# Three more broadcasts of dt per tile in the first and the last block of a state-space and experts kernel

## The chip, the cores and the metric

The kernel runs on one core of a Trainium2 chip. The metric is the device time in microseconds. The engines are TensorE (PE, matmuls; PEld is its weight load), VectorE (DVE), ScalarE (ACT), GpSimd (POOL) and SyncE (SP, which here issues most DMAs). TensorE's clock has two levels, 1.2 and 2.4 GHz; a granted clock of 1.00 in the profile is the higher, 0.50 the lower.

## The reference

For x of 2 x 1024 tokens and 256 channels, with xn = layernorm(x), the result is x + ssm(xn) + ffn(xn).

```
# ssm(x): D = 256 channels, N = 64 states
xn = layernorm(x) * norm_w + norm_b
delta, B, C = split(xn @ x_proj_w.T)
delta = softplus(delta @ dt_proj_w.T + dt_proj_b)          # dt
h[t] = exp(dt[t] * A) * h[t-1] + dt[t] * B[t] * xn[t]       # per channel and state
y[t] = sum over states of h[t] * C[t % 64]
return (y + x * D_param) @ out_proj_w.T
# ffn(x): a shared relu^2 MLP (512) plus 6 of 64 experts per token (relu^2, inner size 128),
# chosen from 4 of 8 groups by sigmoid scores
```

## The kernel before

The recurrence is done by VectorE's scan instruction over 1024 time steps. A **tile** is two channels with their 64 states (128 partitions) and one of the two sequences: 256 tiles in 8 blocks of 32. In `body`, `it` is the block and `s` the tile within it; `c` is a tile that an engine works ahead on. The steps of a tile are:

- TensorE copies the dt of its two channels to all 128 partitions (`bcast_dt`, L1331). dt was split earlier into three bf16 parts. `spread(g, c, bank)` (L1326) multiplies 24 rows of parts (tile PK) by a selection matrix (`sel`) into one PSUM bank of 512 columns; g = 0 and 1 are the two halves of dt's 1024 time steps, g = 2 and 3 those of g = dt * xn. The groups use different quarters of the array's rows. For dt the two halves go to the banks 0 and 1 or 2 and 3, by turns. `bcast_dt` first waits for `scan_done`: the scan of tile c-2 must have left these banks.
- ScalarE makes exp(dt * A) in place there (`decay`, L820).
- TensorE copies g (`bcast_g`) and VectorE multiplies it by B into U (`product`, L1126 for both halves at once, L1131 for one). In blocks 1 to 6 and the first tiles of block 7, three of four products are done by GpSimd instead (L656), with g from DRAM or from ScalarE's copy.
- VectorE scans (L1149) into H and increments `scan_done`.
- After each group of 8 tiles TensorE sums over the states (`y_rows`, L1317, 32 columns of the array each) in three runs of 24, 20 and 20 matmuls, at s % 8 = 1, 3 and 5 of the next group. Each fp32 matmul is two records in the trace.

The order is written out by hand, in straight loops over Python numbers, one instruction stream per engine with semaphores between them. At step s TensorE does `bcast_dt` for tile s+2, then what is due of the experts or of y, then `bcast_g` for tile s+4 (where VectorE does the product), then other work. In block 0 that other work is the shared MLP of `shared_step` (L1232 up-projections, then L1238, L1243 and L1244 for one block of 128 output rows, 14 records) at even s up to 14, while GpSimd issues the rest of 96 indirect DMAs that sort the tokens by expert (`scatter`, L642, three per scan). Blocks 1 to 6 hold the experts' matmuls (L1387, L1395, L1430). In block 7 GpSimd gathers the experts' rows back by 96 indirect DMAs (`gather`, L679), and TensorE and VectorE sum them (`add_row`, L1421; `combine`, L1170; `add_sum`, L1185). The gathers wait for these sums, two to three row blocks back. At the end TensorE projects y (L1446) and the result is stored.

Of the kernel before, what the change touches and what calls it, by code (L numbers as in the profile page):

```python
# [32 lines left out]
BLK = 8  # L33
# [25 lines left out]
PARTS = 3  # L59
ROWS = PARTS * 2 * SUB  # L60
RING = 18


def state_space_and_experts(nc, x, xprojT, dtT, vecs, A_l, outT, gateT, gbias, w_up, w_down, w_exp, out):
# [5 lines left out]
    with ctx:  # L70
# [3 lines left out]
        def sem(name):  # L74
            return ctx.enter_context(nc.semaphore(name))
# [186 lines left out]
        s_y = [sem(f"y_{k}_loaded") for k in ("first_half", "second_half", "last_block", "last_groups")]  # L262
        s_g = [sem(f"rows_gathered{b}") for b in range(RING)]
        s_os = [sem(f"out_stored{b}") for b in range(2)]

        def row(n):

            n %= RING
            return WE[:, n // 4, n % 4 // 2, n % 2 * D:(n % 2 + 1) * D] if n < 12 else XG[:, (n - 12) // 2, n % 2, :]

        def at_least_0(value):

            return max(value, 0) if isinstance(value, int) else value
# [84 lines left out]
        def sums(t):  # L358

            return ps[:, 6, 0:D]  # L360
# [237 lines left out]
        def _(pool):  # L598
# [73 lines left out]
            def gather(n):  # L672
# [4 lines left out]
                elif t >= 3:  # L677
                    pool.wait_ge(comb, added(t - 3, k))
                pool.indirect_dma_start(row(n), None, yg_d,  # L679
                                        bass.IndirectOffsetOnAxis(ap=slot[:, k, t:t + 1].bitcast(u32), axis=0))\  # L680
                    .then_inc(s_g[n % RING], 16)

# [226 lines left out]
        def _(dve):  # L909
# [252 lines left out]
            def combine(t, k):  # L1162

                n = t * TOPK + k
                dve.wait_ge(s_g[n % RING], 16 * (n // RING + 1))
                if t == 0 and k == ON_PE:
# [44 lines left out]
        def _(pe):  # L1211
# [109 lines left out]
            def parts_for(it, c):  # L1321

                q = c // SUB
                pe.wait_ge(s_pk[q % NPK], (it * (SL // SUB // NPK) + q // NPK + 1) * 16)

            def spread(g, c, bank):  # L1326

                return mm(ps[:, bank, :], sel[32 * g:32 * g + ROWS, c % SUB, :],  # L1328
                          PK[32 * g:32 * g + ROWS, c // SUB % NPK, :], start=True, stop=True)

            def bcast_dt(it, c):  # L1331
                parts_for(it, c)
                pe.wait_ge(scan_done, at_least_0(it * SL + c - 1))
                spread(0, c, 2 * (c % 2))
                spread(1, c, 2 * (c % 2) + 1).then_inc(dt_bcast, 1)

# [23 lines left out]
            def body(it, moe):  # L1360
                for s in range(SL):
# [3 lines left out]
                    if not beyond(it, s + DLEAD):  # L1365
                        bcast_dt(it, s + DLEAD)
# [45 lines left out]
            def add_row(t, k):  # L1412
# [6 lines left out]
                pe.wait_ge(scaled_ident, t * ON_PE + k + 1)  # L1419
                pe.wait_ge(s_g[n % RING], 16 * (n // RING + 1))  # L1420
                ins = mm(sums(t), scaled[(t * ON_PE + k) % len(scaled)], row(n), start=(k == 0), stop=(k == ON_PE - 1))  # L1421
# [13 lines left out]
            for c in range(DLEAD):  # L1435
                bcast_dt(0, c)
# [69 lines left out]
```

## Time and profile before

| | us |
|---|---|
| three runs | 1054.78, 1041.98, 1053.79 |
| median | 1053.79 |
| the profiled execution: time | 1045.13 |
| its span | 1043.4 |
| block 0 (first scan at 170.16) | 156 |
| blocks 1 to 6 (326 to 862.4) | 536 |
| block 7 (862.4 to 1016.1) | 154 |

Over the span TensorE is busy for 807.5 us (77%), VectorE for 869.9 us (83%), ScalarE for 576.3 us and GpSimd for 571.3 us. The mean granted clock is 0.838.

In the timelines of the profile a row gives the start, the duration, the engine, the line, the operation, what it writes and reads, and how many instructions were merged; in brackets stands how long the engine was idle before, and what ended it. "issue" is a wait for nothing that the profile shows, "remote" one whose releaser it could not tell. The ends of matmuls are modelled: when a result is really there is told by the engine that waits for it.

### The profile page before, as it was taken

To read this page: it belongs to the slowest core of one execution; us is meant where nothing else is said; L and a number is where in the kernel's file an instruction comes from. 1 tells how busy PE (TensorE), PEld (TensorE's weight loads), DVE (VectorE), ACT (ScalarE), POOL (GpSimd) and SP (SyncE) were. 2 spreads that over 40 slices of the span, in tenths; PEclk is the share of its full clock that TensorE was granted. 3 is DMA by queue.
4 is the path that set the end of the run, shared out by engine and by line. 5 is a ranking of instruction groups with operands and counts; after the bars stand their busy time and mean duration, and the time that the engine had idled before them with its cause. 6 is when DMAs were issued, how large, how long until landed. Compare 5 with 4: busy or idle time off the path is not lost.

```text
span 1043.4 us, 19216 instructions
## 1 busy us (share of the span) xinstructions
PE 807.5 (77%) x6887; PEld 505.5 (48%) x6888; DVE 869.9 (83%) x725; ACT 576.3 (55%) x897; POOL 571.3 (55%) x381
## 2 busy tenths in 40 slices
PE   2967954477445898899998998988896856788788
PEld 3633641144113565566665665665664533344346
DVE  7798899555589999989998998989896999687873
ACT  3552234222225787778777787878785754233440
POOL 5002257554535765756756765756654599555640
PEclk9988985557567999999998999989998967565659
DMA  9579317222535999999999999999999862334322
GB/s 332 188 247 341 113 60 252 86 76 73 166 100 149 255 279 271 276 289 300 293 294 265 279 306 283 271 275 289 268 310 293 230 167 70 96 104 131 99 66 86
DMA packets 178206, 217.33 MB, mean 208 GB/s; under 512 B 50465, under 2 KB 137378, under 8 KB 177890
## 3 DMA queue, kind: packets, MB, share of 16 engines
q1 hardware_dynamic: 168898, 190.93, 64.7%
q0 software_dynamic: 9216, 25.18, 7.8%
q8 instruction: 57, 0.93, 0.4%
q14 instruction: 35, 0.29, 0.1%
HBM read 144.61 MB, written 71.30 MB: 207 GB/s over the span
## 4 chain that ended last, share of the span: by engine, by line
PE 29%; SPq 16%; DVE 12%; issue 11%; DMA 8%; another core or an unknown queue 4%; ACT 3%; POOL 2%; DVEq 0%; ACTq 0%; POOLq 0%
PE ps L1317 11%; DVE H L1149 9%; DMA WE<-w_exp_dram 7%; PE ps L1328 5%; SPq L444 5%; SPq L493 3%; PE ps L1421 3%; SPq L498 3%; PE ps L1387 3%; PE ps L1430 2%; DVE U L1126 2%; ACT ps L820 2%; PE ps L1395 1%; POOL U L656 1%
## 5 line engine op out<-in xcount | busy, mean ns | idle before, releaser
L1149 DVE TENSOR_TENSOR_SCAN H<-ps,U 128x1024 f32<-128x1024 f32 x256 | 581.4, 2284 | 32.6 <-ACT ps L820 27.3
L820 ACT ACTIVATE ps<-ps,Acur 128x1024 f32<-128x1024 f32 x256 | 278.9, 1090 | 263.4 <-PE ps L1328 190.9
L656 POOL TENSOR_TENSOR U<-X,B 128x1024 f32<-128x1024 f32 x100 | 237.2, 2372 | 183.7 <-DMA X<-g_d 126.4
L1328 PE MATMUL ps<-PK,sel 24*128 24x512 bf16 x824 | 153.4, 436 | 146.9 <-DVE H L1149 71.4
L1317 PE MATMUL ps<-H,CB 128*32 128x128 f32 x4096 | 247.7, 395 | 8.7 <-issue 8.5
L1317 PEld LDWEIGHTS ps<-H,CB 128*32 128x32 f32 x4096 | 145.2, 130 | 93.2 <-issue 39.7
L1328 PEld LDWEIGHTS ps<-PK,sel 24*128 24x128 bf16 x824 | 44.1, 93 | 259.5 <-issue 255.1
L642 POOL DMA_INDIRECT xg_d<-XN,slot x96 | 98.3, 1024 | 94.9 <-DVE H L1149 40.4
L1126 DVE TENSOR_TENSOR U<-ps,B 128x1024 f32<-128x1024 f32 x57 | 68.9, 1209 | 77.8 <-remote 45.6
L656 POOL TENSOR_TENSOR U<-GS,B 128x1024 f32<-128x1024 f32 x50 | 119.6, 2391 | 17.4 <-DVE H L1149 13.6
L1387 PE MATMUL ps<-XT,WE 128*128 128x128 f32 x640 | 90.8, 287 | 21.1 <-DMA WE<-w_exp_dram 21.1
L1387 PEld LDWEIGHTS ps<-XT,WE 128*128 128x128 f32 x640 | 86.1, 200 | 31.4 <-issue 28.4
L1430 PE MATMUL ps<-WE,AS 128*128 128x256 f32 x320 | 90.5, 405 | 0.0
L679 POOL DMA_INDIRECT WE<-yg_d,slot x66 | 62.9, 954 | 40.5 <-issue 19.7
L1131 DVE TENSOR_TENSOR U<-ps,B 128x512 f32<-128x512 f32 x98 | 65.5, 668 | 14.7 <-PE ps L1328 14.7
L1430 PEld LDWEIGHTS ps<-WE,AS 128*128 128x128 f32 x320 | 54.2, 189 | 22.3 <-issue 18.1
L872 ACT COPY GS<-ps 128x512 f32<-128x512 f32 x100 | 59.8, 598 | 0.4 <-PE ps L1328 0.4
L1395 PE MATMUL ps<-ident,XG 128*128 128x128 f32 x320 | 53.4, 293 | 6.5 <-ACT YO L891 6.4
L688 POOL TENSOR_TENSOR U<-H,U 128x1024 f32<-128x1024 bf16 x6 | 12.6, 2138 | 81.7 <-DVE H L1057 81.7
L860 ACT ACTIVATE RL<-ps 128x256 f32<-128x256 f32 x80 | 30.8, 385 | 44.4 <-PE ps L1387 44.4
L867 ACT COPY XT<-ps 128x512 f32<-128x512 f32 x80 | 45.8, 573 | 6.3 <-PE ps L1395 5.8
L891 ACT COPY YO<-ps 128x512 f32<-128x512 f32 x80 | 47.4, 592 | 0.0
(185 smaller groups left out, 777.9 us busy)
## 6 DMA issues: line engine op xcount, KB each, us to landing
X<-g_d SPq DMA_DIRECT2D x200, 256.0 KB
WE<-w_exp_dram SPq DMA_DIRECT2D x160, 256.0 KB, 5.0
xg_d<-CB SPq DMA_DIRECT2D x20, 1024.0 KB, 10.6
XG<-xg_d SPq DMA_DIRECT2D x80, 256.0 KB, 6.3
yg_d<-YO SPq DMA_DIRECT2D x80, 256.0 KB, 6.2
PK<-pk_d SPq DMA_DIRECT2D x64, 128.0 KB
pk_d<-H SPq DMA_DIRECT2D x12, 256.0 KB
X<-x_dram SPq DMA_DIRECT2D x4, 512.0 KB, 5.6
```

What stands on the lines that cost most here:

```text
L642: pool.indirect_dma_start(xg_d, bass.IndirectOffsetOnAxis(ap=slot[:, k, t:t + 1].bitcast(u32), axis=0), XN[:, t, :], None).then_inc(scatte ...
L656: nc.gpsimd.tensor_tensor(U[:, c % 4, :], rows, B2[:, b * L:(b + 1) * L], ALU.mult).then_inc(u_pool, 1)
L679: pool.indirect_dma_start(row(n), None, yg_d, bass.IndirectOffsetOnAxis(ap=slot[:, k, t:t + 1].bitcast(u32), axis=0))\
L820: nc.scalar.activation(a_tile(c), a_tile(c), ACT.Exp, scale=Acur[:, b, pair:pair + 1]).then_inc(a_ready, 1)
L1126: V.tensor_tensor(U[:, c % 4, :].rearrange("p (a c) -> p a c", a=2), ps[:, 4:6, :], B2[:, b * L:(b + 1) * L].rearrange("p (a c) -> p a c", ...
L1131: V.tensor_tensor(U[:, c % 4, 512 * k:512 * k + 512], ps[:, 4, :], B2[:, b * L + 512 * k:b * L + 512 * k + 512], ALU.mult).then_inc(g_used, 1)
L1149: V.tensor_tensor_scan(H[:, (s // GRP % 2) * GRP + s % GRP, :], a_tile(s), U[:, s % 4, :], 0.0, ALU.mult, ALU.add).then_inc(scan_done, 1)
L1317: ins = mm(o, CB[:, b, 16 * j + i, :], hb[:, :, :, 16 * j + i], start=(i == 0), stop=(i == 15))
L1328: return mm(ps[:, bank, :], sel[32 * g:32 * g + ROWS, c % SUB, :], PK[32 * g:32 * g + ROWS, c // SUB % NPK, :], start=True, stop=True)
L1387: ins = mm(ps[:, 4, u * P:(u + 1) * P], W1[:, middle % MBUF, u, k, :], XT[:, u, k, :], start=(k == 0), stop=(k == 1))
L1395: ins = nc.tensor.transpose(ps[:, 6, k * P:(k + 1) * P], XG[:, taken % MBUF, k // 2, k % 2 * P:(k % 2 + 1) * P], ident[:, :])
L1430: ins = mm(ps[:, 6, u * D:(u + 1) * D], AS[:, u, :], W2[:, p % MBUF, u, :], start=True, stop=True)
```

## The change

For each tile of `it` 0 and `it` 7, the two matmuls of `bcast_dt` are issued three times more, into the same banks, ahead of the pair that increments `dt_bcast`. Each writes with start and stop set, so the last pair overwrites the earlier ones and the result is the same. `bcast_dt` runs two tiles ahead: through `it` 0 go the tiles 0 to 33, through `it` 7 the block's tiles 2 to 31.

```
+EXTRA = 3
 ...
             def bcast_dt(it, c):
                 parts_for(it, c)
                 pe.wait_ge(scan_done, at_least_0(it * SL + c - 1))
+                if it in (0, BLK - 1):
+                    for _ in range(EXTRA):
+                        spread(0, c, 2 * (c % 2))
+                        spread(1, c, 2 * (c % 2) + 1)
                 spread(0, c, 2 * (c % 2))
                 spread(1, c, 2 * (c % 2) + 1).then_inc(dt_bcast, 1)
```

TensorE's program in block 0 around the first two runs of y, before. The names are the PSUM (ps), the parts of dt and g (PK), the scans' results (H) and the C values (CB):

```order
L1328 MATMUL ps<-PK,sel 128x512 x2
L1317 MATMUL ps<-H,CB 32x128 x24
L1328 MATMUL ps<-PK,sel 128x512 x6
L1238 MATMUL ps<-WE 128x256 x2
L1238 MATMUL ps<-WE,XG 128x256 x2
L1243 MATMUL ps<-dwo,xnT 128x256 x2
L1244 MATMUL ps<-X,ident 128x256
```

And in the changed kernel, whose lines after 61 are one further on, and after 1334 five:

```order
L1329 MATMUL ps<-PK,sel 128x512 x8
L1318 MATMUL ps<-H,CB 32x128 x24
L1329 MATMUL ps<-PK,sel 128x512 x12
L1239 MATMUL ps<-WE 128x256 x2
L1239 MATMUL ps<-WE,XG 128x256 x2
L1244 MATMUL ps<-dwo,xnT 128x256 x2
L1245 MATMUL ps<-X,ident 128x256
```

Nothing has changed its place: the dt pair ahead of the y run is four pairs now, and of the six broadcasts behind it, the two of dt are eight.

## Rows read from the trace of the kernel before

**Rows 1.** Busy time by stage: stretch, its length, busy us (instructions), PEclk, DMA share, GB/s.
```profile
170.00:326.00 156.00, 89.20 (x582) 43.61 (x582) 103.94 (x62) 40.79 (x49) 77.38 (x79) 0.63 0.36 115
326.00:862.40 536.40, 467.53 (x4928) 310.83 (x4925) 491.09 (x289) 401.13 (x633) 347.61 (x154) 0.94 1.00 273
862.40:1016.10 153.70, 116.86 (x746) 59.62 (x747) 121.42 (x104) 59.93 (x103) 94.20 (x92) 0.60 0.34 94
```
**Rows 2.** Timeline, a quiet part of block 0: start, us, engine, line, operation.
```profile
300.18 0.61 PE L1328 MATMUL ps<-PK,sel 24*128 24x512 bf16 x2 [1.59 <-DVE H L1149]
300.83 1.09 ACT L820 ACTIVATE ps<-ps,Acur 128x1024 f32<-128x1024 f32 x1 [3.15 <-PE ps L1328]
...
304.38 2.28 DVE L1149 TENSOR_TENSOR_SCAN H<-ps,U 128x1024 f32<-128x1024 f32 x1
...
307.35 2.83 PE L1317 MATMUL ps<-H,CB 128*32 128x128 f32 x48
...
307.69 2.28 DVE L1149 TENSOR_TENSOR_SCAN H<-ps,U 128x1024 f32<-128x1024 f32 x1
...
310.81 1.23 DVE L1126 TENSOR_TENSOR U<-ps,B 128x1024 f32<-128x1024 f32 x1 [0.83 <-PE ps L1328]
```
**Rows 3.** Waits in 170 to 326: who waited for whom, total, times, longest.
```profile
ACT ps L820 <- remote: 45.4, 7, 13.1
```
**Rows 4.** The same view of 862 to 1016.
```profile
DVE U L1126 <- remote: 12.5, 4, 6.1
```
**Rows 5.** Timeline, block 0 while GpSimd scatters.
```profile
281.15 1.06 PE L1328 MATMUL ps<-PK,sel 24*128 24x512 bf16 x4
...
284.74 0.96 POOL L642 DMA_INDIRECT xg_d<-XN,slot  x1 [0.30 <-issue]
285.63 1.09 ACT L820 ACTIVATE ps<-ps,Acur 128x1024 f32<-128x1024 f32 x1 [5.60 <-remote]
```
**Rows 6.** Timeline, an earlier stretch of block 0, also with scatters.
```profile
218.66 0.39 PE L1328 MATMUL ps<-PK,sel 24*128 24x512 bf16 x2
...
224.44 0.41 PE L1317 MATMUL ps<-H,CB 128*32 128x128 f32 x1 [0.33 <-issue]
...
225.13 0.42 PE L1317 MATMUL ps<-H,CB 128*32 128x128 f32 x1 [0.28 <-issue]
...
226.56 1.09 ACT L820 ACTIVATE ps<-ps,Acur 128x1024 f32<-128x1024 f32 x1 [13.11 <-remote]
```
**Rows 7.** Stretches within runs of scatters: PE and PEld records are the first two counts.
```profile
257.37:269.50 12.13, 7.90 (x69) 4.63 (x68) 9.77 (x6) 3.46 (x4) 9.39 (x10) 0.64 0.72 232
278.42:281.10 2.68, 2.68 (x42) 1.59 (x40) 2.68 (x2) 1.09 (x1) 2.07 (x3) 0.50 0.14 49
```
**Rows 8.** Timeline, four broadcasts (dt and g) at once.
```profile
202.99 0.61 PE L1328 MATMUL ps<-PK,sel 24*128 24x512 bf16 x4
```
**Rows 9.** Timeline of PE, bf16 matmuls of 512 columns at clock 0.50.
```profile
98.70 3.91 PE L1298 MATMUL ps<-H,XT 128*128 128x512 bf16 x9
```
**Rows 10.** The same line in a stretch at clock 1.00.
```profile
102.60:105.20 2.60, 2.60 (x14) 1.08 (x11) 1.00 1.04 340
```
**Rows 11.** Timeline of PE, the shared output row blocks at either clock.
```profile
212.61 2.05 PE L1238 MATMUL ps<-WE 128*128 128x256 f32 x4
...
108.68 1.03 PE L1238 MATMUL ps<-WE 128*128 128x256 f32 x4
```
**Rows 12.** Timeline, the row sums of block 7 at either clock.
```profile
881.71 1.13 PE L1421 MATMUL ps<-WE,RL 128*128 128x256 f32 x4 [0.19 <-DVE XN L1185]
...
952.63 2.08 PE L1421 MATMUL ps<-WE,AS 128*128 128x256 f32 x4
```
**Rows 13.** Timeline, block 0 at clock 1.00, GpSimd scattering until 239.65.
```profile
238.81 0.40 PE L1328 MATMUL ps<-PK,sel 24*128 24x512 bf16 x4
...
241.15 1.09 ACT L820 ACTIVATE ps<-ps,Acur 128x1024 f32<-128x1024 f32 x1 [3.13 <-remote]
```

More of the change, by code:

```diff
@@ L61 @@
 RING = 18
+EXTRA = 3
 def state_space_and_experts(nc, x, xprojT, dtT, vecs, A_l, outT, gateT, gbias, w_up, w_down, w_exp, out):
@@ L1333, in bcast_dt @@
                 pe.wait_ge(scan_done, at_least_0(it * SL + c - 1))
+                if it in (0, BLK - 1):
+                    for _ in range(EXTRA):
+                        spread(0, c, 2 * (c % 2))
+                        spread(1, c, 2 * (c % 2) + 1)
                 spread(0, c, 2 * (c % 2))
```

## The prediction

> **What bounds the kernel now.** I read the three stages first, then the waits of the two outer blocks, then single tiles. The execution that was profiled took 1045.13 us for a span of 1043.4 us, and the sum below starts there. The median of the three times is 1053.79 us, 8.7 us more; their spread is 12.8 us.
>
> The stages differ [rows 1]. From 326 to 862 us (blocks 1 to 6) TensorE's clock is granted at 0.94 on average and VectorE is busy for 491 of 536 us. In block 0 and in block 7, where the change works, the clock is 0.63 and 0.60, and VectorE is busy for 104 of 156 us and for 121 of 154. VectorE does the scans that everything else serves, so about 52 and 32 us of these blocks are waits of the engine that should never wait.
>
> In a quiet part of block 0 there is hardly any [rows 2]: scans start at 304.38 and 307.69, 3.31 us apart, which is a scan and a product. The pair of matmuls that broadcasts dt starts at 300.18, when a scan ends; ScalarE's exp runs on it from 300.83 to 301.92, and the scan that reads it starts at 304.38. That is **2.4 us of slack**. A run of 48 records of y (307.35) costs VectorE 0.83 us there, because the broadcast of g stands behind it (310.81).
>
> The same work goes otherwise while GpSimd issues indirect DMAs. Four broadcasts start at 281.15; ScalarE gets its result at 285.63, almost four microseconds late, just when GpSimd's run of six scatters ends (284.74 + 0.96) [rows 5]. A pair that starts at 218.66 gives its exp at 226.56, and meanwhile TensorE starts single records 0.7 us apart (224.44, 225.13), with nothing shown that it waits for [rows 6]. I call this a **hold**. Seven such waits of ScalarE stand in block 0, up to 13.1 us long [rows 3], and VectorE has four in block 7 [rows 4]: eleven. From the start of a run of indirect DMAs to a hold TensorE starts 42+40 or 69+68 records, matmuls and weight loads together [rows 7], so about 80 to 140. In the quiet part only GpSimd's last three scatters are left and no hold comes. I know no mechanism for it and use the pattern.
>
> **The change, part by part.** It adds 6 matmuls and 6 weight loads to each of 64 tiles (34 through `it` 0, since the broadcast runs two tiles ahead, and 30 through `it` 7): 384 matmuls on the 824 of L1328. It adds no wait, DMA or semaphore, and the programs of the other engines stay as they are. The added ones stand behind the wait for scan_done and ahead of the pair that counts, so all of them lie on the way from scan c-2 to exp c.
>
> *Length of one extra pair.* No row shows a 24-row pair behind another on the same rows of the array. The lower bound is nothing, since four broadcasts take 0.61 us, as two do [rows 2, 8]. The upper bound is a lone pair in full, 0.61 us at the low clock [rows 2] or 0.40 at the high one [rows 13]. Nearest are matmuls of the same 512 bf16 columns back to back: 9 in 3.91 us at the low clock, 0.43 each [rows 9], and 14 in 2.60 us at the high one, 0.19 each [rows 10]. I take 0.43 and 0.2, so three pairs are **1.3 or 0.6 us**.
>
> *Ordinary tiles.* 1.3 us is less than the 2.4 us of slack, so exp c still ends before scan c is due: nothing. Where that cover is gone, in a tile that a hold has delayed already, up to 1.3 us each.
>
> *Tiles with y.* The y records stand behind the longer dt, and behind them the g broadcast that VectorE's product waits for. The 0.83 us above becomes 2.1 us, or 1.4 at the high clock. There are 9 such runs in block 0 and 12 in block 7; 21 times 0.6 to 1.3 is 13 to 27 us if every one showed. In about half of them a hold ends later anyway. I take **+10 us**, ends 0 and 27.
>
> *Holds.* This is the largest term. TensorE starts 582+582 records in block 0 and 746+747 in block 7 [rows 1], 36 and 47 a tile. With 12 more they are a third and a quarter more. If a hold comes after a given number of records within a run of indirect DMAs, 80 to 140 records are now some two to four tiles and then some two to three, and holds come sooner and oftener. Charged in proportion, the waits of 52 and 32 us grow by 17 and 8, 25 us. But a hold ends when GpSimd runs dry, and GpSimd's own work (96 scatters, 96 gathers) stays the same. I take four fifths, **+20 us**. The lower end is 0. The upper end is 67: 12 records at 0.7 us are 8.4 us, on eight of the eleven.
>
> *Clock.* More streaming should raise the granted clock of both blocks. Four records of a shared output row block take 2.05 us at the low clock and 1.03 at the high one [rows 11]; all 14 take 5.9 us at the low clock (212.61 to the next broadcast at 218.66 [rows 6, 11]), so some 3.0 at the high. Four of L1421 take 2.08 or 1.13 us [rows 12]. A hold at the high clock was shorter: broadcasts at 238.81, exp at 241.15, 1.7 us late by the usual 0.65 [rows 13]. I expect the mean clock of the two blocks to go from about 0.62 to about 0.75 and take **-4 us**, ends 0 and -49 (the first rival's savings).
>
> The sum is 10 + 20 - 4 = +26 us: 1045.1 + 26 = 1071 by the profiled execution, 1053.8 + 26 = 1080 by the median. I predict a time between them, **1075 us**.
>
> A rule speaks against that sign. In the trace the clock follows the work: 0.94 where TensorE is busy for 468 of 536 us, 0.63 where it is busy for 89 of 156 [rows 1]. The Trainium skill, page "TensorE: Matmul & The Clock Gate", Part 1 on the clock gate, says that the throttled clock is the default state and that activity releases it. By that rule the added matmuls could pay for themselves, as in the first rival; by the rows the direction agrees.
>
> **The rivals.** *One, the clock pays: the other side, faster.* Its place is both outer blocks, and it decides from a mean granted clock of about 0.9 there. Its price: the four shared row blocks save 2.9 us each and the four pairs of shared up-projections about 1.7 (18 us); twelve L1421 quartets beside y runs save 0.95 each (11); ten holds are 2 us shorter (20). Against that stand 21 y runs at 0.6 (13). That is -36 us: 1009 by the profiled execution, 1018 by the median. For it speaks that the clock has so much room. Against it: the added part is 1.3 us in a tile of 3.3 to 5, and at the high clock only 0.6, so the clock can fall again. Chance 0.12.
>
> *Two, all is hidden.* Holds follow GpSimd's runs alone, the exposed y tiles and the clock cancel: 0 to +12 us, 1045 to 1066. For it: holds end with a run of scatters [rows 5]. Against it: quiet stretches of 17 us inside such a run exist, and the hold comes when many records have gone. Chance 0.28.
>
> *Three, every held tile pays in full.* The 12 new records go at 0.7 us, 8.4 us a hold, and GpSimd does not run dry meanwhile. On eleven holds that is +92: 1137. Against it: the hold of [rows 5] ends with GpSimd's run and so cannot grow. Chance 0.07.
>
> *Four, the added matmuls cost nothing at all,* dropped or overlapped, since they write what the next pair overwrites: 1045 to 1054. But they have the same rows and the same bank. Chance 0.03.
>
> **How the numbers follow.** My forecast, holds that come oftener, has 0.50 and runs from 1055 (the y tiles alone on the profiled time) to 1110 (+56 on the median, holds at two thirds of their upper end and the y tiles). The range holds it and cases two and four whole and leaves out the first rival and the third, 0.19: **1038 to 1110**; 1038 is four below the lowest time shown, for a clock that pays a little. A measurement of this kernel tells about 2%, 21 us, from no change. Slower than 1075 by the median lie 0.42 of my forecast's 0.50 and case three: 0.49. Faster by more than 21 us: the first rival, 0.12. Within: 0.08 + 0.28 + 0.03 = 0.39.
>
> **What would show it.** In the changed profile L1329 is a group of 1208 matmuls. In a quiet part exp starts some 1.9 us after a scan's end instead of 0.9, and the pace stays 3.31. Blocks 1 to 6 stay within 3 us of 536; if they don't, something else moved. Blocks 0 and 7 grow by some 14 and 12 us, with more waits above 3 us for L1329 or "remote", the first of them before 184. Their mean clock is near 0.75. I am wrong if the number and length of those waits fall, or if the clock there is above 0.9. The pattern of holds is wrong if one run of indirect DMAs takes well over 140 records with no hold.

## The result and the profile after

In four runs beside the kernel before, the changed kernel took 1071.18 us in the median (1065.57 to 1079.28), against 1052.76 (1041.98 to 1054.78). That is +18.4 us by the medians, a ratio of 1.0175. The ratio over the fast runs of each kernel is 1.0246, interval 1.0177 to 1.0315, or 19 to 33 us. The changed kernel is slower; whether by more than 2%, four runs each don't tell. The profiled executions differ by 28.8 us in the span (1072.2 against 1043.4).

The stages after, which answer to [rows 1] (stretch, length, then busy us and instructions of PE, PEld, DVE, ACT, POOL, and the granted clock, DMA share, GB/s):

```profile
169.93:336.14 166.21, 114.09 (x774) 51.28 (x774) 104.14 (x62) 40.93 (x49) 77.97 (x79) 0.66 0.34 108
336.14:881.54 545.40, 472.18 (x4925) 312.99 (x4925) 491.53 (x288) 401.78 (x633) 347.00 (x153) 0.93 0.99 268
881.54:1045.45 163.91, 142.78 (x927) 68.25 (x927) 121.95 (x104) 59.78 (x103) 94.23 (x92) 0.60 0.32 88
```

Block 0 has grown by 10.4 us, block 7 by 10.2, and blocks 1 to 6, where nothing was added, by 9.1. TensorE is busy for 51 us more in the two outer blocks (25 and 26) and they lose 20.6. The clock has hardly moved: 0.66 and 0.60, where it was 0.63 and 0.60.

The quiet part of block 0 answers to [rows 2]. Timeline: start, us, engine, line, operation.

```profile
312.43 1.89 PE L1329 MATMUL ps<-PK,sel 24*128 24x512 bf16 x8 [1.42 <-DVE H L1150]
313.31 2.28 DVE L1150 TENSOR_TENSOR_SCAN H<-ps,U 128x1024 f32<-128x1024 f32 x1
314.24 2.83 PE L1318 MATMUL ps<-H,CB 128*32 128x128 f32 x48
314.35 1.09 ACT L821 ACTIVATE ps<-ps,Acur 128x1024 f32<-128x1024 f32 x1 [2.22 <-PE ps L1329]
317.00 1.04 PE L1329 MATMUL ps<-PK,sel 24*128 24x512 bf16 x10
317.50 1.22 DVE L1127 TENSOR_TENSOR U<-ps,B 128x1024 f32<-128x1024 f32 x1 [1.91 <-PE ps L1329]
318.64 2.28 DVE L1150 TENSOR_TENSOR_SCAN H<-ps,U 128x1024 f32<-128x1024 f32 x1
```

Four pairs take 1.89 us where one took 0.61, so an added pair is (1.89 - 0.61) / 3 = 0.43 us. Exp starts 1.92 us after the first of them instead of 0.65. The two scans before that y run are 3.31 us apart (310.00 and 313.31): an ordinary tile pays nothing. The scan behind the y run comes 5.33 us later, and VectorE waits 1.91 us for g where it waited 0.83.

A hold of block 0 with a run of six scatters, to be set beside [rows 5]:

```profile
285.16 1.54 PE L1329 MATMUL ps<-PK,sel 24*128 24x512 bf16 x10
...
287.48 0.96 POOL L643 DMA_INDIRECT xg_d<-XN,slot  x1 [0.30 <-issue]
289.83 1.23 DVE L1127 TENSOR_TENSOR U<-ps,B 128x1024 f32<-128x1024 f32 x1 [5.64 <-remote]
289.85 1.09 ACT L821 ACTIVATE ps<-ps,Acur 128x1024 f32<-128x1024 f32 x1 [5.81 <-remote]
290.97 2.28 DVE L1150 TENSOR_TENSOR_SCAN H<-ps,U 128x1024 f32<-128x1024 f32 x1
```

The run ends at 288.44, and VectorE's product and exp start 1.4 us later; before, exp started with the run's end. The hold still ends with GpSimd, and something is then paid behind it: the first comparison shows what. The waits of block 0 (who waited for whom, total, times, longest), which answer to [rows 3], and after them one of block 7 to [rows 4]:

```profile
ACT ps L821 <- PE ps L1329: 70.9, 20, 8.3
...
DVE U L1127 <- remote: 33.2, 5, 10.0
...
ACT ps L821 <- remote: 27.5, 5, 12.0
ACT ps L821 <- issue: 22.2, 3, 9.7
...
DVE U L1127 <- PE ps L1329: 20.1, 7, 7.7
...
DVE U L1127 <- issue: 7.3, 1, 7.3
```
```profile
DVE U L1127 <- remote: 12.5, 3, 5.0
```

ScalarE's waits for "remote" are 27.5 us in 5 and not 45.4 in 7, but the label alone misleads: with the two other labels ScalarE waits 120.6 us, where it waited 112.5. VectorE's waits are the better measure, since its scans set the pace. Those over 4 us were 50.1 us in 7 in block 0 before, and are 54.2 in 8. In block 7 those over 2.5 us were 18.4 us in 5 and are 20.3 in 5. Holds have grown by some 4 and 2 us, what is paid behind them included, and not by the sum that I charged.

### The profile page after: what moved, and what is told of

It reads as the page before. It is cut to its first block, busy times and chain, and to the rows that moved or that the text cites. A ratio compares the mean times of both kernels' runs of the same rounds, so it can differ in the third digit from the quotient of the medians.

```text
span 1072.2 us, 19984 instructions
## 1 busy us (share of the span) xinstructions
PE 863.9 (81%) x7271; PEld 524.3 (49%) x7272; DVE 871.2 (81%) x725; ACT 577.0 (54%) x897; POOL 571.5 (53%) x381
## 4 chain that ended last, share of the span: by engine, by line
PE 45%; DVE 10%; issue 7%; DMA 6%; SPq 6%; ACT 5%; another core or an unknown queue 3%; POOL 1%; DVEq 0%; ACTq 0%; POOLq 0%
PE ps L1318 16%; PE ps L1329 11%; DVE H L1150 8%; DMA WE<-w_exp_dram 6%; PE ps L1392 4%; PE ps L1426 4%; PE ps L1435 4%; ACT ps L821 3%; PE ps L1400 2%; SPq L445 2%; SPq L499 1%; DVE U L1127 1%; SPq L494 1%; PE ps L1451 1%
## 5 line engine op out<-in xcount | busy, mean ns | idle before, releaser
L1329 PE MATMUL ps<-PK,sel 24*128 24x512 bf16 x1208 | 211.9, 469 | 109.5 <-DVE H L1150 62.4
L1318 PE MATMUL ps<-H,CB 128*32 128x128 f32 x4096 | 249.7, 395 | 10.5 <-issue 10.1
L1329 PEld LDWEIGHTS ps<-PK,sel 24*128 24x128 bf16 x1208 | 62.2, 101 | 245.4 <-issue 234.5
## 6 DMA issues: line engine op xcount, KB each, us to landing
xg_d<-CB SPq DMA_DIRECT2D x20, 1024.0 KB, 10.5
```

Source lines behind the costliest of these rows:

```text
L1318: ins = mm(o, CB[:, b, 16 * j + i, :], hb[:, :, :, 16 * j + i], start=(i == 0), stop=(i == 15))
```

## The experiments

Each comparison ran on one chip beside the kernel before. That kernel took 1043.29 us in the first comparison, near the runs above, but **987.89, 989.71 and 986.50 us in the other three**, each on another chip. This turned out to matter more than most edits. The kernel of before was only timed on those three chips, not profiled. Edits are to the changed kernel. Each stage given below is from that kernel's profiled execution, first scan to first scan.

**First comparison, a chip with holds.** The control (e0) is the program of before.

```
-EXTRA = 3
+EXTRA = 0
```


> The program of before, once more; its profile is the control for the others. If the stages of before repeat, block 0 takes 156 us and block 7 some 154, and the ratio is 1.00. The open point is blocks 1 to 6, which grew from 536 to 545 us in the changed kernel though nothing was added there: if that is the usual scatter of a profile, this one differs from 536 by some 5 to 10 us too; if the change did it, this one is at 536 within 3.

Ratio 0.9988 (0.9947 to 1.0028). In e0 block 0 took 152.1 us, blocks 1 to 6 534.4, block 7 152.2. So an unchanged program moves by 4 us in block 0 and 2 in the others between two profiles.

```
-                if it in (0, BLK - 1):
+                if it == 0:
```


> The added matmuls in block 0 alone. Holds that come oftener: block 0 takes 166 us as in the changed kernel and block 7 takes 154, the ratio is near 1.012 (half of the 1.025). If the growth of blocks 1 to 6 hangs on block 0 (another phase of the transfers), it is here too. If the costs of the two blocks are not additive, this is 1.00 or 1.02.

```
-                if it in (0, BLK - 1):
+                if it == BLK - 1:
```


> The added matmuls in block 7 alone. Holds that come oftener: block 7 takes 164 us as in the changed kernel, block 0 156, the ratio is near 1.012.

Block 0 alone (e1): 1.0122 (1.0070 to 1.0173), as expected. Block 7 alone (e2): 1.0058 (1.0003 to 1.0113), half of what was expected. Its profiled execution took 1060.0 us where its median is 1052.56; in it block 0 took 152.3 us, blocks 1 to 6 549.7 and block 7 159.3, not 164. The stages of block 0 alone:

```profile
169.78:332.19 162.41, 112.20 (x774) 50.19 (x774) 104.20 (x62) 41.04 (x49) 78.16 (x79) 0.67 0.34 111
332.19:877.81 545.62, 474.47 (x4925) 315.44 (x4925) 491.18 (x288) 402.19 (x633) 346.65 (x153) 0.93 1.00 268
877.81:1030.38 152.57, 111.80 (x747) 57.68 (x747) 121.45 (x104) 59.62 (x102) 94.13 (x92) 0.62 0.35 95
```

The added matmuls of block 0 lengthen block 0 (162.4 us against 152.1) and leave block 7 as it was (152.6 against 152.2). The two ratios add up to 1.018, 19 us (11 to 27).

```
+NARROW = 64
-            def spread(g, c, bank):
-                return mm(ps[:, bank, :], sel[...], PK[..., :], start=True, stop=True)
+            def spread(g, c, bank, n=512):
+                return mm(ps[:, bank, 0:n], sel[...], PK[..., 0:n], start=True, stop=True)
-                        spread(0, c, 2 * (c % 2))
-                        spread(1, c, 2 * (c % 2) + 1)
+                        spread(0, c, 2 * (c % 2), NARROW)
+                        spread(1, c, 2 * (c % 2) + 1, NARROW)
```


> The added matmuls of both blocks write 64 columns and not 512: as many records, an eighth of the streaming. Theory A (a hold comes after a number of records within a run of indirect DMAs): the number of records decides, so the holds stay as in the changed kernel, 11 scans of block 0 over 4.5 us apart, and the ratio is 1.015 to 1.025; with less exposed ahead of exp and y it loses at most 10 us of the 20 to 29. Rival B (the length of the added matmuls between a scan's end and exp, and ahead of g, costs the time): 64 columns take an eighth, so the ratio is 1.000 to 1.005, block 0 takes 156 to 158 us.

The narrow kernel (e3): ratio 1.0107 (1.0055 to 1.0159), between the two expectations; block 0 156.7 us, as rival B wrote, block 7 156.0. A y tile shows what the length does (timeline, the wait before g's product):

```profile
309.85 1.22 DVE L1128 TENSOR_TENSOR U<-ps,B 128x1024 f32<-128x1024 f32 x1 [1.01 <-PE ps L1330]
```

VectorE waits 1.01 us, 0.18 more than with no added pair, where wide pairs added 1.08. Length alone would thus give a sixth of the change's cost, some 3 us; the two outer blocks lost 5.8 against the means of the unchanged ones (154.0 and 152.9), and the ratio says 11 (6 to 17). So 3 us or more may hang on the number of records here. Nine scans of block 0 start over 4.5 us apart, where theory A wanted eleven and the kernel of before has seven.

A hold behind y records shows length and number apart. VectorE's product for the step from the scan of tile 20 to the next, in the control, in e1 and in the narrow kernel:

```profile
281.62 1.23 DVE L1127 TENSOR_TENSOR U<-ps,B 128x1024 f32<-128x1024 f32 x1 [4.12 <-remote]
```
```profile
285.50 1.22 DVE L1127 TENSOR_TENSOR U<-ps,B 128x1024 f32<-128x1024 f32 x1 [5.54 <-remote]
```
```profile
284.56 1.22 DVE L1128 TENSOR_TENSOR U<-ps,B 128x1024 f32<-128x1024 f32 x1 [4.14 <-remote]
```

GpSimd's run ends at 281.72, 284.21 and 284.67. With wide pairs the product starts 1.3 us behind that end, with as many narrow ones at it, as in the control. The wide pairs are paid in this hold, and it is their length that is paid. Exp is no such sign: in the narrow kernel too it starts 1.3 us behind the end (285.96).

**Second comparison, and the holds are gone.** The first two kernels leave out the 72 scatters that GpSimd issues in block 0 (only 24 of 96 are made, so most experts work on zeros), without the added broadcasts (f0) and with them (f1).

```
-                        sp.wait_ge(scattered, 16 * TT * TOPK)
+                        sp.wait_ge(scattered, 16 * AHEAD)
 ...
-                        for n in due:
-                            scatter(n)
```


> The program of before without the 72 scatters that GpSimd issues during block 0 (only the first 24 are made, so most experts work on zeros); no added matmuls. Theory A (the waits of block 0 are holds, and a hold needs a run of indirect DMAs): after the first run, which ends near 170, no scan of block 0 waits over 4.5 us; the block takes 108 to 118 us instead of 152 to 156, the ratio is 0.96 to 0.965. Rival B (TensorE's chain itself is too long at the low clock, and the DMAs only stand beside it): block 0 stays over 145 us.

> The same without the 72 scatters, with the three added broadcasts in both outer blocks. Theory A: in block 0 they now cost what they expose at the tiles with y only, 9 times 0.6 to 1.3, so 4 to 11 us over the block 0 of the kernel without both, most likely 6; ordinary scans stay 3.31 apart. Rival C (the added matmuls cost block 0 its 10 to 14 us with or without the DMAs): 10 to 14 us more again. Block 7 still takes 7 to 11 us more.

Without added broadcasts 0.9976 (0.9931 to 1.0021): leaving the scatters out is worth nothing on this chip, and neither theory A's 0.96 nor rival B's long block came. With them 1.0228 (1.0141 to 1.0315). These expectations were written for a chip with holds. Their blocks 0 and 7:

```profile
169.13:285.91 116.78, 82.13 (x582) 40.27 (x582) 103.69 (x63) 40.80 (x49) 8.39 (x7) 0.65 0.24 72
...
825.74:954.29 128.55, 95.80 (x747) 51.23 (x747) 120.96 (x104) 60.09 (x103) 94.19 (x92) 0.75 0.40 113
```
```profile
169.61:293.15 123.54, 97.61 (x774) 44.79 (x774) 103.69 (x63) 41.00 (x49) 9.56 (x7) 0.75 0.24 69
...
827.05:967.28 140.23, 118.92 (x926) 60.21 (x927) 121.71 (x104) 60.03 (x103) 94.21 (x92) 0.72 0.38 104
```

Block 7 has all its gathers in both, and yet takes 128.6 us where it took 152 to 154: 24 us less without any edit there. The change costs 6.8 us in block 0, in theory A's 4 to 11 and below rival C's 10 to 14, and 11.7 in block 7, 18.4 in all.

```
-EXTRA = 3
+EXTRA = 9
```


> Nine added broadcasts of 64 columns in place of three of 512: three times the records, about 1.0 us of length in a tile instead of 1.28 at the low clock (8 narrow matmuls stand 1.1 us ahead of the counted pair's start with 3 pairs, some 0.1 a pair). Theory A (the number of records within a run decides): many more and earlier holds, block 0 over 172 us and block 7 over 168, the ratio 1.035 to 1.06. Rival D (the length decides: a held tile shows the added matmuls in full once the hold ends): at or below the changed kernel, block 0 160 to 166 us, ratio 1.01 to 1.025.

This is the kernel of 64 columns with nine of them (f2). Ratio 1.0105 (1.0018 to 1.0192), block 0 120.3 us, block 7 132.2. Exp starts 1.12 us after the first record instead of 0.65, so nine pairs are 0.47 us long and not the 1.0 that was expected; that came from a row of e3 in which the counted pair was already included. The wait before g's product is 1.11 us, 0.28 more than 0.83. Three times the records cost two fifths of what three wide pairs cost (3.5 + 3.7 against 18.4 us), and their length at exp is two fifths as well (0.47 against 1.27). So without holds the length accounts for the cost, and nothing is left for the number. On a chip with holds it was not run, and both theories were written for one.

```
-AHEAD, PER_SCAN = 24, 3
+AHEAD, PER_SCAN = 32, 2
```


> No added matmuls. 32 scatters are issued ahead of block 0 and then two after each scan, where it was 24 and three. Theory A (a hold comes in an unbroken run and lasts until it ends): the first run is 10 us longer, so the first hold ends near 200, but afterwards two scatters take 2.3 of a scan's 3.31 us and the run breaks each time, so the holds are few or short; block 0 takes 135 to 148 us, ratio 0.985 to 0.995. Rival E (holds follow the amount of indirect DMAs and not the unbroken run): block 0 takes 150 us or more, ratio 1.00 to 1.01.

This kernel (f3) has no added broadcasts. Ratio 1.0196 (1.0094 to 1.0297); block 0 took 115.1 us, blocks 1 to 6 547.4, block 7 130.1. There was no hold to shorten, so it says nothing on theory A or rival E. What the profile shows of the loss is mostly block 1, 94.7 us against 85.0 in f0: the last scatter is issued at 293.8, SyncE waits 11.2 us for the scatters, and behind that wait in its queue stand the loads of g, for which GpSimd then waits 8.9 us.

**Third comparison, also without holds.** The added broadcasts split by what stands behind them.

```
+                y_behind = it in (0, BLK - 1) and it * SL + c - DLEAD >= GRP and (c - DLEAD) % GRP in YPART
-                if it in (0, BLK - 1):
+                if it in (0, BLK - 1) and not y_behind:
```


> The three added broadcasts only in the 43 tiles behind whose dt no matmuls of y stand; 258 of the 384 added matmuls. The runs on the second chip showed the whole cost of the change (1.0228 against 0.9976) where no holds are to be seen, at the scans that follow matmuls of y. Theory F (the cost is what the 21 tiles with y expose; elsewhere the slack of a scan hides it): ratio 1.000 to 1.006, at most 6 us. Theory A (holds that come oftener with the number of records, on a chip that has them): two thirds of the records, so two thirds of the growth from holds, ratio 1.010 to 1.016 on such a chip and 1.000 to 1.006 on one without holds.

The second has `and y_behind` instead.

> The complement: the three added broadcasts only in the 21 tiles behind whose dt stand matmuls of y; 126 of the 384. Theory F: nearly the whole cost of the change, 21 times 0.6 to 1.3 us, so 13 to 21 us, ratio 1.014 to 1.022. Theory A: one third of the records, a third of the growth from holds and the exposed part that was put at 10 us, ratio 1.010 to 1.016.

In the 43 tiles without y (g1): 1.0002 (0.9956 to 1.0048). In the 21 tiles with y (g2): 1.0218 (1.0137 to 1.0299). **A third of the added matmuls carries the whole cost, and two thirds cost nothing that the times show.** Both ratios are as theory F wrote; theory A allows 1.000 to 1.006 for the first on such a chip too, and the second interval only touches its 1.010 to 1.016. Blocks 0 and 7, first without y, then with y only:

```profile
169.59:289.10 119.51, 95.57 (x720) 45.30 (x720) 104.12 (x62) 40.72 (x49) 78.70 (x79) 0.71 0.47 150
...
826.01:954.71 128.70, 107.14 (x855) 55.31 (x855) 120.98 (x104) 59.98 (x103) 94.23 (x92) 0.75 0.40 113
```
```profile
169.78:295.34 125.56, 86.98 (x636) 42.34 (x636) 103.78 (x63) 40.80 (x49) 77.34 (x79) 0.70 0.44 143
...
831.12:974.52 143.40, 111.63 (x818) 57.37 (x819) 121.66 (x104) 60.03 (x103) 94.25 (x92) 0.69 0.37 102
```

In the profile the 43 tiles are not quite free. Block 0 takes 119.5 us, 2.7 more than in f0. The steps from the scans of tiles 2, 4, 6, 8 and 10 are longer by 1.2, 0.7, 0.3, 0.3 and 0.6 us, and the last step of the block by 1.3; one step with shared matmuls is 1.7 shorter at a higher clock.

**Fourth comparison.** The kernel without scatters (h1) and the changed kernel (h2), on one more chip.

> The kernel of f0 again: the program of before without the 72 scatters of block 0, since the chip of the first try had no holds even in kernels with all scatters. On a chip with holds (the kernel of before takes some 1040 us): theory A, a hold needs the indirect DMAs beside it, so block 0 takes 108 to 120 us instead of 152 to 156 and the ratio is 0.955 to 0.975; the rival, that such a chip runs TensorE's chain slower whatever GpSimd does, leaves block 0 over 145 us and the ratio at 1.00. On a chip without holds the ratio is 1.00 as before, and the question stays open.

> The changed kernel itself once more, on the same chip as the one above. On a chip without holds: theory F (the cost is what the 21 tiles with y expose) gives 1.018 to 1.025, 18 to 25 us on 988, block 7 about 141 us; theory A, by which four fifths of the cost are holds, gives at most 1.010. On a chip with holds: 1.018 to 1.032 as in the comparison already shown; block 0 some 162 to 166 us.

It had no holds either. Without scatters 1.0047 (0.9984 to 1.0111), block 0 116.8 us, block 7 131.0. So whether a hold needs the indirect DMAs stays open. The changed kernel: 1.0139 (1.0045 to 1.0232), between theory F's 1.018 and theory A's 1.010, and the interval holds both; block 7, 141.2 us, is as theory F wrote. Its stages:

```profile
170.16:294.23 124.07, 99.12 (x774) 45.19 (x774) 104.02 (x62) 40.90 (x49) 78.62 (x79) 0.73 0.45 145
294.23:834.14 539.91, 471.48 (x4927) 312.89 (x4925) 491.14 (x289) 401.84 (x633) 346.14 (x153) 0.93 1.00 271
834.14:975.38 141.24, 121.22 (x926) 61.11 (x927) 121.53 (x104) 60.05 (x103) 94.39 (x92) 0.71 0.37 103
138.30:262.00 123.70, 88.48 (x610) 43.63 (x610) 108.22 (x77) 48.69 (x57) 95.42 (x93) 0.75 0.47 157
```

The last row is one unbroken run of 93 indirect DMAs, in which TensorE gets through 610 matmuls and 610 weight loads. The prediction called its pattern of holds wrong if one run took well over 140 records with no hold: on this chip it is wrong. A y tile within it:

```profile
215.43 1.04 PE L1329 MATMUL ps<-PK,sel 24*128 24x512 bf16 x8
...
216.40 2.36 PE L1318 MATMUL ps<-H,CB 128*32 128x128 f32 x40
...
218.69 1.04 PE L1329 MATMUL ps<-PK,sel 24*128 24x512 bf16 x10
219.09 0.96 POOL L643 DMA_INDIRECT xg_d<-XN,slot  x1 [0.30 <-issue]
219.19 1.22 DVE L1127 TENSOR_TENSOR U<-ps,B 128x1024 f32<-128x1024 f32 x1 [1.94 <-PE ps L1329]
```

GpSimd issues without a pause and g still arrives 0.5 us after its matmul starts.

## Why the prediction was right in its number and wrong in its terms

The outer blocks, us. "With" is three wide broadcasts in that block. Left out are the narrow and the split kernels, and e2, whose profiled execution was a long one.

| | without | with | difference |
|---|---|---|---|
| block 0, holds | 155.9, 152.1 | 166.2, 162.4 | +10.3 |
| block 7, holds | 153.8, 152.2, 152.6 | 163.9 | +11.0 |
| block 0, no holds | 116.8, 116.8 (no scatters), 115.1 (f3) | 123.5 (no scatters), 124.1 | +7.6 |
| block 7, no holds | 128.6, 131.0, 130.1 | 140.2, 141.2 | +10.8 |

The change costs 21 us in the profiles with holds and 18 in those without. With the blocks of e2 (152.3 without, 159.3 with) it would be 20 with holds. By the times it is 18 (medians) or 26 (ratio) in the first measurement, 19 in e1 and e2 together, and on chips without holds 14 (4 to 23) and 25 (1.0139, and 1.0228 over 0.9976). No profile shows the kernel of before itself on a chip without holds: two of the three for block 0 leave out scatters, and the third makes them two at a time.

*Length of a pair.* Right: 0.43 at the low clock; at the high one (1.04 - 0.39) / 3 = 0.22, where I had 0.2. Exp 1.9 us after the first broadcast, and the pace of 3.31 us, came as written. The 43 ordinary tiles cost nothing in the times (g1). One kind pays in the profiles, at the end of block 0, where GpSimd makes the products and scans follow each other every 2.2 us: there the slack is smaller than three pairs, and the scan waits for exp itself.

```profile
336.14 2.29 DVE L1150 TENSOR_TENSOR_SCAN H<-ps,U 128x1024 f32<-128x1024 f32 x1 [1.25 <-ACT ps L821]
```

The prediction took its 2.4 us of slack for all tiles.

*Tiles with y, +10.* **This term was too small.** The whole cost without holds is some 18 us by the profiles, and g1 and g2 put it on the tiles with y: 21.6 us by the ratio of g2 (14 to 30), in the upper half of the 0 to 27 that I had worked out. I had halved it because a hold would end later anyway. The distances from one scan to the next in block 0, from the scans' starts, show where that is so:

| from scan of tile | 10 | 12 | 14 | 18 | 20 | 22 | 26 | 28 | 30 |
|---|---|---|---|---|---|---|---|---|---|
| no holds, without (f0) | 6.8 | 6.4 | 6.4 | 4.3 | 3.8 | 3.8 | 4.3 | 3.7 | 2.2 |
| no holds, with (h2) | 7.8 | 5.4 | 5.4 | 4.8 | 5.1 | 5.1 | 5.5 | 5.1 | 3.3 |
| holds, without (e0) | 14.2 | 9.0 | 9.1 | 10.5 | 7.5 | 7.5 | 4.3 | 3.8 | 2.2 |
| holds, with (e1) | 10.8 | 9.1 | 9.1 | 9.2 | 9.0 | 9.0 | 5.5 | 5.1 | 3.3 |
| holds, narrow (e3) | 11.1 | 9.1 | 9.1 | 8.8 | 7.6 | 7.6 | 4.4 | 4.0 | 2.2 |

The last five steps grow by 6.6 us with holds, by 6.5 without, and by 0.5 with narrow pairs. Two of the five are held (20 and 22), and the hold covers nothing there. Steps 12, 14 and 18 together get shorter, by 1.3 us with holds and 1.5 without.

*Holds, +20.* **This is the step that failed.** What I charged, more waits with more records, is 3 us by the table, and 3 to 8 by the narrow kernel; a block moves by up to 4 us between two profiles of one program, so even this is not clear of noise. The first hold does come earlier, as written, in tile 2 instead of tile 4. But the sum hardly grows. With the added matmuls in block 0 alone (e1) the distances from the scans of tiles 2, 4, 7 and 10 are 12.5, 3.6, 8.2 and 10.8 us, 35.1 in all; in the control they are 3.3, 12.2, 3.3 and 14.2, 33.0 in all. In block 7 of the changed kernel the held steps move a tile ahead in the same way. The prediction itself said that a hold ends when GpSimd runs dry and that GpSimd's own work stays the same, and took a fifth off for it; that deserved nearly all. Scans over 4.5 us apart are 11 and not 7 in block 0, but that count, which e3's expectation had named as the sign of more holds, is no such sign: without holds it goes from 3 (f0) to 8 (h2). The blocks grew by 10 and 10 us and not by 14 and 12.

*Clock, -4.* Small, as taken, but for another reason. With holds it hardly rose (0.66 and 0.60, not 0.75). Without them block 0 was at 0.65, 0.64 and 0.71 without added broadcasts and at 0.75 and 0.73 with them, and there it paid: four records of the shared row blocks ahead of the y runs of tiles 12 and 14 took 2.08 and 1.70 us in f0 and 1.13 in h2, and each of the two steps came down by 1.0 us. Block 7 was at 0.75, 0.71 and 0.72 without and at 0.72 and 0.71 with them. The prediction had set a rule of the Trainium skill, page "TensorE: Matmul & The Clock Gate", Part 1 on the clock gate, against its sign: activity releases the clock. The mean clock agrees with it in block 0 of the chips without holds and shows nothing of it in block 7. The first rival, which needed 0.9, had no ground in either. One of its readings was off: the 14 records take 6.05 us from 212.61 to 218.66, not 5.9.

*Blocks 1 to 6 within 3 us.* Wrong for the profile (+9.1), and only in part explained. With holds the two unchanged profiles have 536.3 and 534.4 us there, and the four with added matmuls 545.4, 545.6 (e1), 549.7 (e2) and 544.5 (e3). Yet in e2 nothing is added before block 7, so added matmuls that run can't have lengthened these blocks. On chips without holds it is the other way about: 530.4 to 539.9 in five profiles with added matmuls, 539.8, 543.3 and 547.4 in three without. Some 9 of the profile's 28.8 us lie in these blocks, and their cause stays open.

The rivals: "all is hidden" was right on the holds and wrong on the y tiles; "every held tile pays in full" was right for the held y tiles 20 and 22, but the price is the 1.3 us of the pairs, not 12 records at 0.7. The fourth, that the added matmuls cost nothing at all, was wrong: L1329 is a group of 1208, each pair with its 0.43 us.

So 1075 was near 1071 by luck: the errors of two terms cancelled, and about 18 for tiles with y and 3 for holds stand where I had 10 and 20.

## What to carry to other kernels

Work that is added ahead of a producer costs next to nothing where the consumer has slack, and up to its whole length where a second product stands behind it in the same queue. Count those places first, measure the slack at each kind of tile, and don't halve the count because something else is late there. A wait that ends with another engine's run goes by that engine's work: here added work moved the waits and made their sum only some 2 to 4 us longer. Before a mechanism is made from one chip's profile, run the unchanged kernel on another and profile it there: here 55 us of 1043 differed from chip to chip.

## What the hardware showed unasked

On the chip of the first comparison, and in the profiles of before and after, some of TensorE's results in a run of indirect DMAs reach other engines only about when the run ends, from 0.4 us before its end to a few us behind it. On three other chips no profile has anything of the kind. The changed kernel, the one program profiled on both sorts, shows it best: 610 matmuls pass in one run of 93 indirect DMAs, block 0 takes 124.1 us instead of 166.2 and block 7 141.2 instead of 163.9, 65 of the 70 us between the two spans. The kernel of before, not profiled there, differs by 55 us in its times. The prediction's 80 to 140 records up to a hold are a trait of those chips or of their condition at the time; which of the two, and what holds the results, no run here tells. A pair of broadcasts with 64 columns costs 0.47 / 9 = 0.05 us, with 512 columns 0.43 at the low clock.
